# Two layers of a graph network on one core: layer 0's units cut to two blocks from block 28 on, two visits in a quad, a ring of 12 slots at the end, and the update's transfers on ScalarE's queue

## The reference

```
# layer 0
m   = silu([x[src], x[dst], e] @ mW1 + mb1) @ mW2 + mb2
agg = segment_sum(m, dst)
h   = silu([x, agg] @ uW1 + ub1) @ uW2 + ub2
x1  = layernorm(x + layernorm_affine(x + h))
# layer 1
agg = segment_sum(x1[src], dst) / max(degree, 1)
h   = relu(relu([x1, agg] @ W1 + b1) @ W2 + b2)
out = layernorm(x1 + h)
```

## Time and profile before

| | us |
|---|---|
| median of 3 runs | 2191.05 |
| range of the runs | 2190.15 to 2192.39 |
| the profiled execution, its own time | 2192.59 |
| its span, first to last instruction | 2190.8 |
| busy: PE, DVE, POOL, ACT | 1967.6, 1631.8, 1519.4, 1411.4 |

### The profile page before, as it was taken

How to read it: one execution, slowest core, us unless ns; L and a number is a source line. 1 busy time by engine, 2 the same in 40 slices (tenths; PEclk the granted TensorE clock), 3 DMA queues, 4 the chain that set the end, 5 groups by cost and what they waited for, 6 DMA issues and landing times.

```text
span 2190.8 us, 58541 instructions
## 1 busy us (share of the span) xinstructions
PE 1967.6 (90%) x19638; PEld 1740.5 (79%) x19638; DVE 1631.8 (74%) x5459; ACT 1411.4 (64%) x3734; POOL 1519.4 (69%) x1605
## 2 busy tenths in 40 slices
PE   7898988988898998899899999899998999999686
PEld 7887777777786787787798797788898788999575
DVE  8697877877687877877777877878777878886343
ACT  3686766766586766776766766766766766775132
POOL 7477777777777777777777777777777777774010
PEclk9997988998998999998999999999999999999899
DMA  8476576685676686686788686787888687887775
GB/s 293 130 236 194 164 215 190 186 243 169 194 228 198 186 251 198 183 264 185 226 254 254 205 270 195 236 265 228 258 248 247 200 279 242 276 255 228 221 246 165
DMA packets 285033, 487.73 MB, mean 223 GB/s; under 512 B 118330, under 2 KB 143164, under 8 KB 284728
## 3 DMA queue, kind: packets, MB, share of 16 engines
q1 hardware_dynamic: 233278, 378.15, 55.0%
q0 software_dynamic: 50016, 102.53, 17.9%
q10 hardware_dynamic: 1434, 3.25, 0.4%
HBM read 375.62 MB, written 108.13 MB: 221 GB/s over the span
## 4 chain that ended last, share of the span: by engine, by line
POOL 53%; issue 25%; DMA 8%; PE 6%; DVE 5%; ACT 1%; DVEq 0%; SPq 0%; ACTq 0%; POOLq 0%
POOL gath L839 53%; DMA gath<-P_d,src_i 7%; PE ps_pre L1099 2%; DVE edgeK L898 1%; PE ps_cnt L1116 1%; DVE pre L911 1%; PE ps_p L382 1%; POOL sumT L846 1%; DVE edgeL L896 1%; PE ps_sum L1136 1%; PE ps_l L1152 0%; ACT counts L1255 0%; PE ps_pre L1101 0%; DMA Q_d<-Qst 0%; DMA A_d<-counts 0%
## 5 line engine op out<-in xcount | busy, mean ns | idle before, releaser
L839 POOL DMA_INDIRECT gath<-P_d,src_i x1535 | 1460.0, 951 | 490.8 <-issue 456.1
L898 DVE TENSOR_SCALAR edgeK<-iotaK,key 128x500 bf16<-128x500 f16 (+1 forms) x1564 | 666.6, 486 | 0.0
L1099 PE MATMUL ps_pre<-wc,eT_c 128*128 128x128 f32 x3128 | 618.5, 320 | 1.1 <-ACT gath L1266 1.1
L1116 PE MATMUL ps_cnt<-edgeK,edgeL 128*128 128x250 bf16 (+1 forms) x3128 | 487.7, 304 | 72.9 <-DVE edgeK L898 60.7
L911 DVE TENSOR_TENSOR pre<-ps_pre,gath 128x512 f32<-128x512 f32 x384 | 261.7, 681 | 363.6 <-DMA gath<-P_d,src_i 321.6
L1099 PEld LDWEIGHTS ps_pre<-wc,eT_c 128*128 128x128 f32 x3128 | 512.0, 205 | 24.0 <-issue 1.5
L1295 ACT ACTIVATE h<-pre 128x512 f32<-128x512 f32 x391 | 245.4, 628 | 431.4 <-DVE pre L911 424.2
L1136 PE MATMUL ps_sum<-edgeN,h 128*128 128x40 f32 x3128 | 421.4, 285 | 80.7 <-ACT h L1295 80.3
L1136 PEld LDWEIGHTS ps_sum<-edgeN,h 128*128 128x128 f32 x3128 | 392.0, 196 | 106.0 <-ACT h L1295 93.1
L1255 ACT ACTIVATE counts<-ps_cnt 128x1000 bf16<-128x1000 f32 x391 | 402.7, 1030 | 56.1 <-PE ps_cnt L1122 42.5
L1116 PEld LDWEIGHTS ps_cnt<-edgeK,edgeL 128*128 128x128 bf16 x3128 | 290.6, 102 | 144.9 <-DVE edgeK L898 72.5
(11 more groups left out here) (154 smaller groups left out, 1467.5 us busy)
## 6 DMA issues: line engine op xcount, KB each, us to landing
eT_c<-eT SPq DMA_DIRECT2D x196, 512.0 KB
A_d<-counts SPq DMA_DIRECT2D x168, 384.0 KB
rel_c<-rel_d SPq DMA_DIRECT2D x196, 240.0 KB
A_v<-A_d SPq DMA_DIRECT2D x85, 448.0 KB
gath<-P_d,src_i POOLq DMA_INDIRECT x1535
A_d<-counts SPq DMA_DIRECT2D x56, 416.0 KB
A_v<-A_d SPq DMA_DIRECT2D x87, 256.0 KB
Qw<-Q_d SPq DMA_DIRECT2D x56, 180.0 KB
```

The costliest lines, as they stand in the source:

```text
L839: pool.indirect_dma_start(gath[:, q, t * D:(t + 1) * D], None, v["P_d"], bass.IndirectOffsetOnAxis(ap=src_i[g % 2][:, c:c + 1], axis=0)).t ...
L898: last = V.tensor_scalar(edgeK[x][:, ROFF[j]:ROFF[j] + A2 * w], iotaK[j][:, :, 0:A2 * w // KR], key[k][:, q * QT + j:q * QT + j + 1], None ...
L1099: T.matmul(o, eT_c[c % RE][:, e0:e0 + P], wc[:], start=True, stop=False)
L1116: last = T.matmul(o[:, :, w0:w0 + w], edgeL[x][:, j, 0:P], r, start=(j == 0), stop=(j == QT - 1 and q == 0), skip_group_check=True)
```

## The change

Three things are changed together.

1. From block 28 (`FINE_B`) on, a unit has two blocks and not four, so there are 17 units and not 13, and x1 is ready in finer steps. The last one, at quad 392, stays.
2. `plan_visits` may put two visits of together 14 blocks into a quad below 392, and takes visits from 4 blocks up there (8 before). A quad's two visits lie side by side in one bank, and DVE's adds wait for the later of the two. By the two plans there are 398 visits in place of 263. Before quad 391 they take 2202 blocks in 319 visits (before: 1988 in 185), 118 quads among them have two, in quads 391 to 400 there are 66 blocks (124), in quads 401 to 452 there are 280 (436), and from 453 on 196 in both.
3. At the end the ring of slots has 12 and not 6 (the six added ones lie in `counts`), and a load is issued up to 10 quads ahead (`AHEAD`), never before the visit that had its slot is through. Before the end there are still four slots, so a visit's load in a run of quads with two visits is issued two quads ahead. The loads and stores of the update go from ACT's queue in place of SP's: the first three at quad 402, the store right behind ACT's scaling (step 6), and behind it the loads of the third update after it.

```
-        hi = min(lo + UB, LAST_B)
+        hi = min(lo + (2 if lo >= FINE_B else UB), LAST_B)
...
+        left = VB
+        for _ in range(2 if s < QUADS else 1):
...
+                n = min(ready - done[d], left)
+                if n >= (4 if s < QUADS - 2 * GQ else 1) and (best is None or n > best[0] and ready < NB):
...
-VB, RA, RT, LEAD = 14, 4, 6, 4
+VB, RA, RT, LEAD, AHEAD = 14, 4, 12, 4, 10
...
+        last = max(last, s - (AHEAD if s >= QUADS + AHEAD + LEAD else LEAD),
+                   -1 if BEFORE[i] is None else VISITS[BEFORE[i]][0])
+        at.setdefault(last, []).append(i)
...
-            dve.wait_ge(l1_mm, i + 1)
+            dve.wait_ge(l1_mm, VISITS_AT[VISITS[i][0]][-1] + 1)
...
                 last.then_inc(l_norm, 1)
+                act.wait_ge(l_norm, w + 1)
+                act.dma_start(v["out"][last_columns(w)[0], :].rearrange("(j p) n -> p j n", p=P),
+                              z[:, 0:n, :]).then_inc(l_out[w % 3], 16)
+                if w + 3 < len(LAST_UNITS):
+                    load_last(w + 3)
```

More of the change, by code:

```diff
@@ L145, in changes_of_sums @@
             at["sums", s // GQ - 1] = n
-        if s - 1 in VISIT_AT:
+        for i in VISITS_AT.get(s - 1, ()):
             n += 1
-            at["visit", VISIT_AT[s - 1]] = n
+            at["visit", i] = n
         if UNIT_AT.get(s, (0, 0))[1] == 1:
@@ L630, in build_edges @@
     A_v += [edgeK[k][:, 0:VB * P] for k in range(2)]
+    A_v += [counts[k][:].rearrange("p a d -> p (a d)")[:, j * VB * P:(j + 1) * VB * P] for k in range(2) for j in range(3)]
     xT_l, x_l = [gath[:, i, :] for i in range(3)], [gath[:, 3 + i, :] for i in range(3)]
@@ L797, in fast @@
                 unit_degrees(s)
[L798 to L799 removed]
+                for i in LOADS_AT.get(s, ()):
+                    load_visit(i)
                 if s == GQ:
                     load_weights(nc, sp, v)
[L802 to L808 removed]
             for k in range(2):
@@ L1234, in fast @@
                 unit_step(s)
-                if s in VISIT_AT:
-                    visit(VISIT_AT[s])
+                for i in VISITS_AT.get(s, ()):
+                    visit(i)
                 last_step(s)
@@ L1378, in fast @@
                 unit_step(s)
+                if s == UNITS[-1][2] + U_LEN + 1:
+                    for w in range(3):
+                        load_last(w)
                 last_step(s)
```

98 lines of the change are left out of this document (50 added, 48 removed).

## The result

| | before | after |
|---|---|---|
| median of 11 runs each, side by side | 2191.49 | 2185.12 |
| range | 2188.44 to 2194.43 | 2181.03 to 2190.59 |
| the profiled execution, its own time | 2192.59 | 2182.88 |
| its span | 2190.8 | 2181.1 |

The ratio is 0.9971, 95% interval 0.9962 to 0.998: 6.4 us faster, where 18.4 were forecast and 2160 was the low and 2184 the high end of the range. The two profiled executions are 9.7 us apart, so 3.3 us of what the traces show is the luck of two single executions.

The account below looks back on a forecast made before the run. POOL was taken as the clock up to about 2004 us, then a tail limited by PE, DVE and chains. Terms -0.4 - 4.6 - 6.4 - 7 = -18.4 us gave 2172.6 against the median 2191.05, range 2160 to 2184.

Parts of the forecast that it names:

- POOL as the clock: Up to about 2004 us POOL's gathers set the pace, 5.0 us a quad; PE, DVE and ACT may run some 20 late.
- Before quad 391: no change: Stretch before the tail: 214 more blocks, 22.5 us of PE, fit without cost; taken as 0, bounds -2 and +3 us.
- I cost it at 0: Before quad 391: double quads' loads, issued two quads ahead, some 9 us before their visits, were to cost nothing.
- rival D: Before quad 391: loads two quads ahead late by 2 us a quad, moving the whole tail, 2197 us; chance 0.06.
- The last unit: Chain of PE, ACT and DVE steps from 2017.5 to 2042.1: -4.6 us through smaller visits, despite a new stall at visit 396.
- To update 0: From the last unit to the end of the first update's second product: -6.4 us, with the product waiting for its input.
- what held PE at 2057 falls away: Ahead of the first update: the 3.6 us wait for a load of counts goes, since SP no longer waits for the store.
- the forecast's order of limits: Ahead of the first update: PE would be ready at 2043 but wait for its input, with the product at 2047.
- The ten intervals: Between updates, 2064.3 to 2153.3: 89 us become 82, so -7, bounds -12 and 0; DVE's step 3 limits smaller visits.
- I add 4 us: In the intervals between updates: allowance for half clock from PE's added idle time, raising 78 us to 82.
- C: Tail held by its chains: x1's store and input as slow, stall at 396, clock drops in most intervals; 2183, chance 0.2.

Follow-up runs that it names:

- transfers alone: Only the change's third part (ring of 12 slots, update's transfers on ACT's queue) on the kernel before: 2188.79 against 2195.6, ratio 0.9963; on a slow chip 0.9985.
- one slot a quad: The change, with both visits of a quad in one slot and loads four quads ahead: 2177.4 against 2195.6 for the kernel before, 0.9916; slow chip 1.0079.
- four banks: Visits from quad 402 rotate over four PSUM banks, added to one slot a quad with the ring started at slot 4: 1.0088 against the kernel before, slow chip.

## Why the prediction was wrong

**POOL as the clock: right.** The waits for DVE stayed under 0.3 us and the last gather came 2.9 us earlier, a little outside the 2 allowed.

**"Before quad 391: no change": the first step that failed.** It took 0, with +3 as the worst, and the unit started 6.4 us later behind the last gather. Two things were wrong. The first is the size: lateness was to be made up in single-visit quads, and eight double quads at 0.3 us were to add at most 3. In the traces the two kernels with the new plan are 3.4 and 4.1 us later over quads 360 to 380, and 4.8 at quad 380 with the change. The second is what it was measured from. The lag of 6.3 us in the earlier trace rows is not a property of the kernel: with the same work transfers alone has 11.4. The lag hangs on landings near the end, of a gather at quad 382 and of a store ahead of DVE's clear, with too few quads behind them to make it good. How the 6.4 us divide between the two can't be told from one trace each. That the store's landing is what delays the clear is read from rows; the edit that would have shown it ran only where it can't be seen.

**"I cost it at 0": loads two quads ahead.** They were late five times, by 1.7 to 2.3 us each: rival D's mechanism at a quarter of the price that it needed (which it worked out for 22 double quads from 345 to 380; the plan has 24). POOL did not wait for it; the landings of 3.4 and 5.6 us in the earlier trace rows, from the tail, were no measure for a queue of pairs. But the last of the five stands just ahead of the stretch that counts:

```profile
1971.76 1.64 PE L1159 MATMUL ps_l<-A_v,x1h 128*128 128x120 bf16 x28 [1.71 <-DMA A_v<-A_d]
```

SP issues the next load behind this visit, at 1973.4, and the last store behind that. And one slot a quad, which takes these waits away, came out at 0.9916 where the change had 0.9971, 18 us, as much as was forecast here. It also halves the stall at 396, and the two were timed on two chips, so what the term of 0 should have been is open.

**The last unit: -3.1 for -4.6.** The mechanism was right, the stall at 396 was 2.42 us and in the chain; without it the unit took 18.3 to 19.5 us in place of 19.6 to 21.7. What the term had at nothing is the clock: it was granted in full in the unit before, at half around the stall after, and the visits behind the stall took 5.1 us, by my estimate from the earlier trace rows 2.4 more than at full clock.

**To update 0: -7.6 for -6.4.** The size was right, the reason partly wrong. Input load 4.2 us behind the store: forecast 5. But "what held PE at 2057 falls away" did not hold: loads into `counts` held it, since visits up to 405 are still loaded four quads ahead. With those gone it waits for the input after all, 5.7 us, so the forecast's order of limits is true one step further.

**The ten intervals: -2.2 for -7, the second step that failed, in its last term.** By the mean of all traces it is -4.0, so a part of the miss is the draw of two executions. The chain through DVE's step 3 is as forecast: more banks change the intervals by 3.5 to 4.1 us and leave PE waiting. What was mis-sized is "I add 4 us" for the clock: over the 78 us of the forecast's chain the trace has 8.8, and the mean of thirteen 7.2. In these thirteen traces, of the new plan with two banks, the intervals go with the clock: 83.9 to 84.2 at 0.92, 84.1 to 85.6 at 0.90, 85.9 to 86.8 at 0.88, 88.6 at 0.87. Between 0.92 and 0.88 a hundredth costs 0.6 us; carried on to the 0.96 of before, that is 82 as an estimate, what was forecast. No run held the clock and changed the work, so that it is the clock alone is argued. The rows at 2070 show how: the idle time that fewer blocks leave is followed by half-clock products, which stand in the chain. The Trainium skill's page "TensorE: Matmul & The Clock Gate", section "HAM oscillation — how this bites in real kernels", has the engine's gaps themselves, waits for DMA there, as the cause of such swings. The rows at 2070 go with that, with 2.2 us of waiting, here for DVE, ahead of a product at 2.02 in place of 1.0 us.

**The rivals.** C (2183) came nearest: the clock in most intervals, and the stall at 396 in the unit. Its third part, a store and input as slow as before, did not happen. Transfers alone and the whole change differ by less than their intervals (0.9963 and 0.9971), though the traces have the change 10 us ahead from the unit's first product on. These traces can't say where that went: of transfers alone the profiled execution is 3.8 us above its median, of the change 2.2 below, and the former span is as long as that of before, 2190.8, though its median is 6.8 better.

## What to carry to other kernels

A lag read from one execution is one draw: before it carries a term, read it over some twenty quads, ask which single landing it hangs on, and whether there is time left behind it to make it good. Work taken from a chain-bound stretch buys idle time, and here idle time on PE went with half clock inside the same chain; it is worth trying to shorten the chain first (four banks gave 3.5 to 4.1 us), and then to take work out. When one resource serves two visits of a quad, give the pair one slot: the lead in quads, not the number of slots, is what the load needs.

## What the hardware showed that I had not expected

The same kernel takes 2191 to 2196 us on some chips and 3076 to 3111 on others, and the order of the versions turns with it: the change and one slot a quad are gains with POOL as the clock, and the versions with the new plan and all its blocks are a loss of 0.4 to 1.1% where PE is late. There PE issues single matmuls 1.4 us apart for up to 19 us. The Trainium skill's page "Runtime: NRT & Kernel Launch", section "Instruction fetch mechanics", has the fetch of straight-line code mostly hidden behind execution. Whether these stretches are a fetch that is not hidden no run here tells; in the 19 us above the two instruction queues moved one packet each. Nor does any run tell what differs between the chips. One landing can decide the start of the tail: the same store took 9.5 us to the clear that waits for it in one execution and 11.3 to 11.9 in three others.
